# Half of the shared experts behind the sorted tiles, with the first gathers there; ternary weights loaded during the attention ahead

## What is computed

```python
def _L1_xattn_ref(q, k, v):        # 8 heads of 16 channels; the keys are the context's columns
    qk = einsum('bdm,bdn->bmn', qh, kh) * scale
    ret = einsum('bmn,bcn->bcm', softmax(qk), vh)
def _L1_ffn_ref(x, w1, g1, w2, g2, w3, g3):      # H = 1024
    _ternary_quant(w): s = mean(abs(w)); round(tanh(w / (s + EPS))) * arctanh(s)
    _linear_bit(x, w, g) = einsum('bsd,od->bso', _act_quant(_rmsnorm(x, g)), _ternary_quant(w))
    h = silu(_linear_bit(x, w1, g1)) * _linear_bit(x, w2, g2)
    return _linear_bit(h, w3, g3)
def _L2_ffn_ref(...):              # E = 16 experts, TOPK = 4, I = 176, shared width 352
    ...
    top_w, top_i = top_k(softmax(x2 @ gate_w.T), TOPK)          # weights scaled to a sum of 1
    routed = sum over the 4 experts e of a token: weight * (silu(x2 @ w1g[e]) * (x2 @ w1u[e])) @ w2[e]
    shared = silu(sg) * su @ sh_down_w.T
    return hid + (routed + shared)
def _L3_xattn_ref(inputs_q, inputs_kv, Wq, Wk, Wv, Wo):         # 16 heads of 128
```

## Time and profile before

| | |
|---|---|
| median of 3 runs | 2105.93 us (2102.1 to 2106.78) |
| the profiled execution | 2107.05 us, of which the span of its instructions is 2105.3 |
| busy share of the span | TensorE 77%, VectorE 66%, ScalarE 39%, GpSimd 30% |
| L1 attention | 395.6 to 513.6 us |
| L1 feed-forward | 514.4 to 669.2 us |
| L2 experts | 1521.1 to about 1764 us |
| L3 attention and feed-forward | 1764.4 to 2105.3 us |

### The profile page before, as it was taken

The page is one execution under the profiler, slowest core; times in us unless marked ns, Lnnn a source line. Parts: engine busy times, 40 slices in busy tenths (PEclk is TensorE's granted clock), DMA queues, the critical chain, the costliest instruction groups (busy, mean ns, idle before and its releaser), DMA issues. The chain is left out here.

```text
span 2105.3 us, 29671 instructions
## 1 busy us (share of the span) xinstructions
PE 1612.0 (77%) x9237; PEld 1138.7 (54%) x9318; DVE 1386.2 (66%) x3775; ACT 815.5 (39%) x2357; POOL 624.6 (30%) x744
## 2 busy tenths in 40 slices
PE   3559988696243888898889599999785995887774
PEld 2324434364121466666666488888653553776763
DVE  6779968587775688888888346455364332567765
ACT  2114444355121566666667233333300221344441
POOL 0020011365201777787776210000043002511100
PEclk8579999788565899999999799999978997999996
DMA  1206610002652900000000500000052225221100
GB/s 60 105 5 181 195 49 1 1 1 76 33 123 86 311 1 1 1 2 1 1 1 1 176 15 15 1 1 1 17 207 68 89 88 212 93 73 66 63 26 8
DMA packets 104405, 129.33 MB, mean 61 GB/s; under 512 B 14208, under 2 KB 89184, under 8 KB 101056
## 3 DMA queue, kind: packets, MB, share of 16 engines
q1 hardware_dynamic: 95264, 112.39, 16.6%
q0 software_dynamic: 8992, 15.08, 3.4%
HBM read 85.75 MB, written 46.94 MB: 63 GB/s over the span
## 5 line engine op out<-in xcount | busy, mean ns | idle before, releaser
L580 POOL TENSOR_TENSOR l0f_diag<-g_identb,l0f_mask 128x1024 bf16<-128x1024 bf16 x16 | 32.0, 2023 | 226.4 <-PE l0f_psA L836 209.8
L2750 ACT ACTIVATE l2x_probs<-l2x_psS,l2x_nmax 128x128 f32<-128x128 f32 x256 | 90.7, 371 | 10.2 <-DVE l2x_nmax L2664 9.9
L2534 POOL TENSOR_TENSOR l2x_probs<-l2x_probs,l2x_rtotal 128x512 f32<-128x512 f32 x64 | 66.8, 1043 | 90.2 <-DVE l2x_rtotal L2670 90.2
L3241 DVE COPY moe_xgT<-moe_psX 128x256 f32<-128x256 f32 x47 | 19.9, 424 | 100.1 <-PE moe_psX L3349 100.1
L2545 POOL TENSOR_TENSOR l2x_vsm<-l2x_vraw,l2x_smooth_row 128x512 f32<-128x512 f32 x64 | 84.7, 1344 | 3.7 <-ACT l2x_vraw L2784 3.4
L3110 POOL MEMSET moe_before<- 128x256 f32 x1 | 0.3, 316 | 287.3 <-POOLq L162 287.3
L2072 POOL DMA_INDIRECT l3a_routed<-rows,slots_slot_of x32 | 31.0, 968 | 174.7 <-issue 166.2
L2895 PEld LDWEIGHTS l2x_psS<-l2x_kT,l2x_qT 128*128 128x128 f32 x512 | 66.8, 191 | 21.9 <-issue 17.7
L996 ACT ACTIVATE l1a_probs<-l1a_psS,l1a_nmax 128x256 f32<-128x256 f32 x128 | 58.8, 473 | 43.9 <-PE l1a_psT L1024 37.0
L819 PE MATMUL l0f_psH<-l0f_wT,l0f_xm 128*128 128x512 bf16 x256 | 68.0, 389 | 10.2 <-DVE l0f_h L660 9.0
L921 POOL TENSOR_TENSOR l1a_probs<-l1a_probs,l1a_rtotal 128x512 f32<-128x512 f32 x64 | 65.1, 1039 | 32.7 <-DVE l1a_rtotal L958 32.7
(11 more groups left out here) (534 smaller groups left out, 4879.7 us busy)
## 6 DMA issues: line engine op xcount, KB each, us to landing
rows<-l2x_zero SPq DMA_DIRECT2D x1, 18304.0 KB, 59.9
kT_ctx<-l0f_held SPq DMA_DIRECT2D x32, 256.0 KB, 3.5
v_ctx<-l0f_held SPq DMA_DIRECT2D x32, 256.0 KB, 3.6
l3a_kT<-kT_ctx SPq DMA_DIRECT2D x8, 1024.0 KB, 5.1
l3a_v<-v_ctx SPq DMA_DIRECT2D x8, 1024.0 KB, 5.6
l0f_wrow<-in_L_ffn_w SPq DMA_DIRECT2D x24, 256.0 KB, 3.0
moe_xg<-rows SPq DMA_DIRECT2D x47, 128.0 KB, 2.0
rows<-moe_yg SPq DMA_DIRECT2D x47, 128.0 KB, 1.7
```

Source lines behind the costliest of these rows:

```text
L2534: nc.gpsimd.tensor_tensor(probs[:, n % 2, :, :], probs[:, n % 2, :, :], rtotal[:, n % 2, :].unsqueeze(2).to_broadcast([P, 4, P]), ALU.mult)\
L2750: last = nc.scalar.activation(probs[:, n % 2, j, :], psS[:, j, :], ACT.Exp, bias=nmax[:, n % 2, j:j + 1], scale=1.0, accum_out=total[:, n ...
```

## The change

- `TernaryWeights` loads the three L1 weights and gains from SyncE during the L1 attention, and ScalarE takes the sums of |w| there, ahead of iterations 8, 12 and 16 (Abs with an accumulator).
- In the L1 attention the zero fill of `vs` comes behind `keys(1)`, and the copies of the values into iteration 1 of ScalarE; TensorE waits for them in iteration 3.
- In the L1 feed-forward VectorE takes the totals and the first ternary weight between statistics and scaling, the second behind it, the third behind the variance for rrms; ScalarE takes the logarithm first. In the steps `add(b-1)` stands inside `quantise_hidden(b)`, before the wait for `rh`.
- In the experts 8 shared units (`AHEAD`) run before the tiles and 8 behind them; routing has 2 units for each group. GpSimd waits for the stores instead of SyncE, and gathers sequences 0 and 1 still in this stage; VectorE multiplies and adds those of sequence 0 at its end.
- The gathered rows and their semaphores (`Routed`) are kept over both stages. The L3 attention gathers from sequence 2 on, one sequence earlier against its mixing.

```diff
+class TernaryWeights:
...
+    SUMS_AT = (8, 12, 16)
...
+    def load(self, sp, A):
+        for j, (name, chunks) in enumerate((("L1_w1T", KC), ("L1_w2T", KC), ("L1_w3T", H1 // P))):
+            sp.dma_start(self.w[j][:, :].rearrange("p (c o) -> p c o", c=chunks),
+                         A[name].rearrange("(c p) o -> p c o", p=P)).then_inc(self.loaded[j], 16)
...
+        sp.wait_ge(self.gains_loaded, 48)
...
+    def sum(self, nc, act, n):
+        if n in self.SUMS_AT:
+            j = self.SUMS_AT.index(n)
+            act.wait_ge(self.loaded[j], 16)
+            wait(act, self.summed, j)
+            nc.scalar.activation(self.magnitude[:, :], self.w[j][:, :], ACT.Abs, accum_out=self.asum[:, j:j + 1])\
+                .then_inc(self.summed, 1)
...
+            @block.sync
+            def _(sp):
+                V.load(sp, A)
...
-                nc.gpsimd.memset(vs[:, :, :, :, :], 0.0).then_inc(zeroed, 1)
...
                 keys(0)
                 keys(1)
+                nc.gpsimd.memset(vs[:, :, :, :, :], 0.0).then_inc(zeroed, 1)
...
-                act.wait_ge(zeroed, 1)
-                for s in range(2):
...
+                def spread_values():
+                    act.wait_ge(zeroed, 1)
+                    for s in range(2):
+                        heads = lambda t: t.rearrange("p c b (g s k) -> p (c b) g s k", s=2, k=HD)[:, :, :, s, :]
+                        nc.scalar.copy(heads(vs[:, s, :, :, :]), heads(G.ctxT[:, :, :, :])).then_inc(vs_made, 1)
...
                 for n in range(N):
                     u = n % 2
+                    V.sum(nc, act, n)
+                    if n == 1:
+                        spread_values()
                     wait(act, turned, 2 * (n - 1))
...
-                    if n == 0:
+                    if n == 3:
                         pe.wait_ge(vs_made, 2)
...
             @block.sync
             def _(sp):
-                for j, (name, chunks) in enumerate((("L1_w1T", KC), ("L1_w2T", KC), ("L1_w3T", HC))):
-                    sp.dma_start(w[j][:, :].rearrange("p (c o) -> p c o", c=chunks),
-                                 A[name].rearrange("(c p) o -> p c o", p=P)).then_inc(loaded, 16)
...
-                sp.wait_ge(loaded, 96)
                 W.load(sp, A)
...
             def _(dve):
                 T.order = o = Order(dve, order)
-                normalise_all(nc, G, T, xn)
-
-                dve.wait_ge(loaded, 96)
-                for j in range(3):
...
+                for b in range(B):
...
+                nc.vector.tensor_scalar(T.ve[:, :], T.mv[:, :, 1], 1e-5, None, ALU.add).then_inc(T.var_ready, 1)
                 dve.wait_ge(totals, 1)
...
                 nc.vector.tensor_tensor(ratio[:, :], up1[:, :], down1[:, :], ALU.mult).then_inc(ratio_ready, 1)
-                for j in range(3):
+
+                def ternary(j):
                     o.step(nc.vector.tensor_scalar(below[:, :], w[j][:, :], nthr[:, j:j + 1], None, ALU.is_lt))
...
                     ins.then_inc(tern_ready, 1)
                     dve.wait_ge(tern_ready, j + 1)
+
+                ternary(0)
+                dve.wait_ge(T.rstd_ready, 1)
+                for b in range(B):
+                    last = nc.vector.tensor_scalar(xn[:, b, :], G.x[:, b, :], T.mv[:, b, 0:1], T.rstd[:, b:b + 1],
+                                                   ALU.subtract, ALU.mult)
+                last.then_inc(T.ln_ready, 1)
+                ternary(1)
                 dve.wait_ge(atanh_ready, 1)
                 o.step(nc.vector.tensor_scalar(atanh[:, :], atanh[:, :], 0.5, None, ALU.mult))
                 dve.wait_ge(squared, 1)
                 nc.vector.tensor_scalar(vrms[:, :], ss[:, :], 1.0 / D, eps, ALU.mult, ALU.add).then_inc(ms_ready, 1)
+                ternary(2)
                 dve.wait_ge(rrms_ready, 1)
...
                     dve.wait_ge(h_squared, b + 1)
                     nc.vector.tensor_scalar(vh[:, u:u + 1], hh[:, u:u + 1], 1.0 / H1, eps, ALU.mult, ALU.add)\
                         .then_inc(vh_ready, 1)
+                    if not is_zero(b):
+                        add(b - 1, 1 - u)
                     dve.wait_ge(rh_ready, b + 1)
...
                 def step(b, u, next_one):
                     gate(b, u)
-                    if not is_zero(b):
-                        add(b - 1, 1 - u)
                     if two_follow(b, next_one):
                         first(b + 2, u)
...
             def _(act):
+                act.wait_ge(ratio_ready, 1)
+                nc.scalar.activation(atanh[:, :], ratio[:, :], ACT.Ln).then_inc(atanh_ready, 1)
...
                 nc.scalar.copy(square[:, 0:1], ss[:, 0:1]).then_inc(squared, 1)
-                act.wait_ge(ratio_ready, 1)
-                nc.scalar.activation(atanh[:, :], ratio[:, :], ACT.Ln).then_inc(atanh_ready, 1)
...
-                pe.wait_ge(summed, 1)
                 nc.tensor.matmul(psO[:, 0:3], G.ones[:, :], asum[:, :], start=True, stop=True).then_inc(totals, 1)
...
-                    o = Order(pool, pool_order)
...
-                    gather(0)
-                    gather(1)
-                    for b in range(2):
-                        pool.wait_ge(first_mixed, b + 1)
-                        gather(b + 2)
-                        invert(b)
-                    mix(2)
+                    invert(0)
+                    R.gather(G, 2)
+                    invert(1)
+                    R.gather(G, 3)
+                    R.mix_on_gpsimd(pool, G, 2)
+                    R.gather(G, 4)
                     for b in range(B):
                         if b + 2 < B:
                             invert(b + 2)
                         if b > 0:
                             side.on_gpsimd(pool, G, b - 1)
                         if b + 3 < B:
-                            mix(b + 3)
+                            R.mix_on_gpsimd(pool, G, b + 3)
+                        if b + 5 < B:
+                            R.gather(G, b + 5)
...
                 def stats(b):
                     if causal:
                         return
-                    if b < 2:
-                        dve.wait_ge(gathered[b], 16 * TOP2)
-                        for k in range(TOP2):
...
-                            if k < TOP2 - 1:
...
-                        dve.wait_ge(mixed, b - 1)
+                    if b == 1:
+                        R.mix_on_vector(dve, G, 1)
+                        dve.wait_ge(R.mixed_first, 2)
+                    elif b >= 2:
+                        dve.wait_ge(R.mixed, b - 1)
...
+def stages_l1_l2_xattn(nc, G, A):
...
-        stage_l1_ffn(nc, G, A, W)
+        with ExitStack() as held:
+            V = TernaryWeights(nc, held)
+            stage_l1_xattn(nc, G, A, V)
+            stage_l1_ffn(nc, G, A, W, V)
...
-        STEP = SHARED // GROUPS
+        AHEAD = 2 * 4
+        STEP = AHEAD // GROUPS
...
+        tile_at = lambda m: m - AHEAD if AHEAD <= m < AHEAD + TILES else None
+        result_at = lambda m: m // 2 if m < AHEAD else min(m - AHEAD, TILES) + AHEAD // 2 + max(m - AHEAD - TILES, 0) // 2
+        half_at = lambda m: m if m < AHEAD else m - TILES if m >= AHEAD + TILES else None
...
-                for u in range(NY):
-                    sp.wait_ge(stored[u], 16 * len(range(u, TILES, NY)))
...
+                for u in range(NY):
+                    pool.wait_ge(stored[u], 16 * len(range(u, TILES, NY)))
+                R.gather(G, 0)
+                R.gather(G, 1)
...
-                def add_shared(b):
-                    dve.wait_ge(down_done, 2 * b + 2)
-                    nc.vector.tensor_tensor(G.x[:, b, :], G.x[:, b, :], psY[b % 2][:, 0:D], ALU.add)\
+                def add_shared(m):
+                    b = half_at(m) // 2
+                    dve.wait_ge(down_done, m + 1)
+                    nc.vector.tensor_tensor(G.x[:, b, :], G.x[:, b, :], psY[result_at(m) % 2][:, 0:D], ALU.add)\
                         .then_inc(shared_added, 1)
...
                 def route(m):
...
                             assign(g - 1)
                         if g < GROUPS:
                             compare(g)
+                            break_ties(g)
                         else:
...
-                    elif j == 1 and g < GROUPS:
-                        break_ties(g)
-                    elif j == 2 and g < GROUPS:
+                    elif g < GROUPS:
                         choose(g)
...
-                for m in range(UNITS + 1):
-                    if m <= SHARED:
+                for m in range(UNITS + 2):
...
-                    if SHARED <= m < UNITS - 1:
-                        if m == SHARED:
-                            copy_tokens(0)
-                        copy_tokens(m + 1 - SHARED)
...
+                    if AHEAD <= m < AHEAD + TILES - 1:
+                        copy_tokens(m + 1 - AHEAD)
...
-                    if m >= 3 and m % 2 and m < SHARED + 3:
-                        add_shared((m - 3) // 2)
```

(34 more changed lines are left out.)

170 lines of the change are left out of this document (78 added, 92 removed).

## The result

The changed kernel takes 2076.64 us (median, 2073.26 to 2077.97), against 2104.79 for the kernel before in the same comparison: ratio 0.9865, 95% interval 0.9848 to 0.9882, about 28 us less. The forecast was 2072, its range 2062 to 2084. The profiled execution has a span of 2075.3 us, 30.0 less than before.

What follows compares the result with a forecast made beforehand. No single bound was taken: TensorE, VectorE, program-order chains and waits bound different stretches. -3.5 - 14.4 - 18.3 + 1.0 + 1.2 = -34.0 us from 2107.05 gave 2073.1, or 2072 against the median; range 2062 to 2084.

Steps and rivals of the forecast that it cites:

- part 1: L1 attention: zero fill moved behind keys(1) on GpSimd, so rstd and the first query come sooner; gain 3.5 us.
- part 2: L1 attention: early weight loads and three ScalarE sums of about 2.1 us each, nearly all hidden; cost 0 to 1.
- Rival C: L1 attention: the sums stall it, by table loads or all their length; +6 to 7 us, 2079, chance 0.06.
- part 3: Start of the L1 feed-forward: VectorE's new order hides waits for rstd and rrms; gain 14.4 us, bounds 13 to 15.
- part 4: L1 feed-forward steps: first(b+2) fills the add's wait for TensorE; gain 18.3 us, bounds 13 to 19.
- rival D: L1 feed-forward steps: TensorE's output or the silu is late in the new order; +17 us, 2089, chance 0.05.
- part 5: Stage seams: two further semaphore groups cleared on their own, 0.5 us each; cost 1.0 us.
- part 6: Experts to L3 attention: first tile 10.4 us sooner, last tile to first score 11.6 us longer; together +1.2 us.
- the wait for weights that was named: L3 attention's head: the fourth piece of query weights lands at S + 16.6, first score at S + 23.
- rival B: Experts' routing: TensorE falls to 1.2 GHz and the scatters starve as before; +7 us, 2079, chance 0.14.
- the forecast of +1.2: Experts and L3 head together: 10.4 us gained up to the first tile, 11.6 lost from last tile to first score.
- Rivals A and E: A: last attention's head shorter, 4 to 8 us less, chance 0.17; E: L1 attention's TensorE clock never rises, +51, 0.03.

Runs made afterwards that it cites:

- e11: e7 with the gather of sequence 1 moved from the experts' stage to the start of L3: 2067.93 us, ratio 0.9813 to the kernel before.
- e7: Changed kernel with zeros by ScalarE, first two L3 query weight pieces loaded early, 12 shared units ahead and 4 behind: 2061.61 us, ratio 0.9783 to before.

## Why the prediction was right, and where it was wrong

**Zero fill (part 1): wrong.** The step that failed is "GpSimd's next work wants the engine at about 408: free". I had looked at GpSimd's queue only. What ran on VectorE in those microseconds was the scaling, and it stood still for 3.46 of the 3.51 us, so that the 3.5 us won in front of it were given back in it. Zeros by ScalarE give them, and two fills cost twice as much. The Trainium skill has the rule: "SBUF — State Buffer", "SBUF: two separate sides", calls the second port pair, which VectorE and GpSimd share, an exclusive lock that a GpSimd instruction, or a VectorE instruction in a 2-port mode or (against a GpSimd instruction that reads SBUF) with two inputs in SBUF, holds for its whole length, while the other blocks. The three durations agree with it; in which mode the scaling runs, the trace does not say. I had not weighed it, though it speaks against just this move. The copies of the values cost nothing, as said.

**Sums (part 2): right.** 1.92 us and 0.21 for reading the total, where 2.1 was estimated; cost 0.0 between executions of like clock (the experts' part alone, without the sums, took 100.1 us from first Exp to last add, the changed kernel, measured again, 99.7). Rival C did not occur: there is no table load. The rule of the Trainium skill ("ScalarE: Activation LUTs", "Table sets: the hidden batching unit") that abs is in every table set agrees with the trace here.

**Start of the feed-forward (part 3): right,** 14.7 against 14.4, step by step, with the new wait at 0.87 instead of 0.9. Of it 0.37 goes again before the first gate.

**The add (part 4): right,** 19.2 against 18.3. The pitch came to 10.7, not 10.9: of the wait for rh 0.27 is left. The silu is not late; rival D is out.

**Barriers (part 5): right,** 0.41 at the one that can be read by itself.

**Experts (part 6).** Last tile to S was forecast at 31.4 and is 30.4 to 31.4 in eight profiles; S to first score at 23, measured 21.2 to 23.6, with the wait for weights that was named. Two terms were off. The gain up to the first tile, forecast at 10.4, is 9.1 in the profile, and by other terms than forecast: the first group's slots came 6.1 us sooner (GpSimd's longest wait fell from 24.8 to 18.8) instead of 2.8, but 3.3 of the 7.6 us of later waits were left. Over eight profiles with 8 units ahead the stretch takes 80.1 to 84.0 us against 89.97, 6.0 to 9.9 less (92.4 in the L1 part alone, where the experts are as before). Where it is short, the slots of the groups come every 8.1 to 9.0 us (changed kernel again), which is the forecast of part 6; where it is long, one group takes up to 16.1 us (1525.58 to 1541.69 with zeros by ScalarE) and the scatters wait 3.5 to 5.0 us for slots behind the first group. That is the effect of rival B, in part of the executions and at about 4 us instead of 7. That the clock makes the difference is not shown: TensorE was granted 0.79 in this group of 16.1 us and 0.83 over the three short ones. And the sum ended at the first score, as if what follows were unchanged. It is 1.5 to 4.2 us longer (309.3 to 312.0 against 307.8). Of that 1.3 looks like the mechanism of part 1 once more, though no run was made for it alone: VectorE's normalisation of the first probabilities takes 2.0 us instead of 0.69 in all eight profiles in which a product of 1.88 us of GpSimd's mixing lies beside it (the six above and the two that have only 12 or 16 units ahead), and in none of the six others; TensorE then waits 2.6 to 3.5 us for it instead of 1.7. In two of the six, the first profile among them, TensorE also runs the next products at 1.2 GHz (1.12 us for 0.66). The rest was not followed. A sum that stops at an event must say that the engines stand there as they did before. So the forecast of +1.2 was too small, by 2.4 us if the means of the profiles are taken; the pair of profiles (+1.26) seemed to confirm it, and only the repeated ones and the time of the experts' part alone (1 to 9 us slower) show that it didn't.

**The sum.** -34.0 forecast, -30.0 in the profile. The zero fill is 3.5 of the difference, the part behind the first score 2.1, 2.2 come in front of all that was changed, in L0, and 1.7 are missing up to the first gate and the first tile; the steps, the start of the feed-forward, the L2 attentions, the tiles and the way from last tile to first score gave 5.5 more. These 5.5 are luck: without them the forecast would have been off by 9.5 us and not by 4.0. Rivals A and E did not occur: the first projection ran at 1.2 GHz, and the clock of the L1 attention rose as before.

## What to carry to other kernels

Before an instruction is moved on GpSimd, look at what VectorE does at its new place, and the other way round, not only at the queue it leaves; here ScalarE took the fill and the copies without cost. In a chain that runs through one engine in program order, a short operation that waits belongs behind independent work of the same engine that is as long as its wait: that single edit gave 19 of 28 us. The units pulled out from beside the routing came back at full price behind the tiles, and TensorE's granted clock fell where they had been (0.50 to 0.81 in the first profile, 1.00 before): this half of the change cost 1 to 9 us by its times, 3.6 in the mean of the profiles. It also made GpSimd's mixing meet VectorE's first normalisation (2.02 us for 0.69): when a change shifts whole stretches, ask which operations of these two engines meet at the new times.

## What the runs showed of the hardware

Stretches with the same code differ between executions by whole steps, with TensorE's clock. First Exp to last add of the L1 attention takes 99.7 to 100.2, 103.8 to 103.9 or 109.0 to 109.1 us, whichever kernel it is. The two tables of stretches are of the changed kernel, measured again, and of `e11`, from the first Exp on (columns as above):

```profile
409.48:429.48 20.00, 17.45 (x106) 11.38 (x107) 13.66 (x27) 13.38 (x50) 11.11 (x12) 0.64 0.00 1
429.48:439.48 10.00, 9.37 (x80) 6.47 (x78) 8.89 (x18) 8.82 (x31) 7.83 (x9) 1.00 0.01 2
```

```profile
404.16:424.16 20.00, 17.93 (x82) 12.13 (x84) 12.15 (x24) 9.86 (x41) 9.83 (x11) 0.50 0.09 34
424.16:434.16 10.00, 10.00 (x52) 6.33 (x52) 6.00 (x12) 4.18 (x19) 5.29 (x8) 0.50 0.00 0
```

In the first 2.4 GHz is granted within 20 us of the first Exp, in the second not within 30; TensorE was busy 17.5 and 17.9 us of the first 20. L0 from its feed-forward's start on, untouched by any edit, takes 310.8 to 317.3 us. So one profile against another is good to some 2 to 9 us where the clock is on the move, and to 0.05 us where it is not.

From the end of the last gather's issue on GpSimd to the first instruction of the next stage pass 4.6 us (12 units ahead; 4.7 with 16, and in `e7`), though no engine has an instruction there; where the gathers end early, the seam takes 1.3. What the 4.6 us consist of is not shown. With 12 ahead VectorE can use the rows of the first four gathers 1.8 us behind the end of the fourth issue, so landing is some part of it.
